# A two-part network on one core: the 32 left-over tokens as the first expert tile, in full fp32 in four strips of one bank, with a new written-out order of all engines' work

## The reference, cut to what matters

```python
x = x + conv_block(layernorm_over_channels(x), ...)      # space gate from Gs, channel gate from Gc
t = tokens(x)                                            # 784 tokens of 128 channels per image
def ffn(x, router_w, router_b, expert_w, expert_b):      # x: layernorm of t
    router_probs = softmax(x @ router_w + router_b)
    top_p, top_i = top_k(router_probs, 2)
    top_p = top_p / sum(top_p)
    expert_out = einsum('bnd,edc->bnec', x, expert_w) + expert_b     # 8 experts, 128 -> 128
    return sum over the two chosen of top_p * expert_out
t = t + ffn(...)
```

## Time and profile before

| what | before |
|---|---|
| median of 3 runs | 1960.88 us (1959.79 to 1966.5) |
| the profiled execution | 1958.27 us, its span 1956.5 us |
| granted TensorE clock, mean | 0.986 |
| busy: PE, PEld | 1779.4 us (91%), 1301.2 us (67%) |
| busy: DVE, ACT, POOL | 1502.8 us (77%), 1195.2 us (61%), 1131.6 us (58%) |
| DVE idle before the first gate of a unit, in the step shown below | 3.04 us |

### The profile page before, as it was taken

One profiled execution on the slowest core, in us unless ns is written; L12 is line 12 of the kernel. 1 busy time (PEld: TensorE's weight loads), 2 busy tenths in 40 slices (PEclk: granted clock), 3 DMA queues, 4 the chain that ended last, 5 costly groups with the idle time before them and its releaser, 6 DMA issues.

```text
span 1956.5 us, 38711 instructions
## 1 busy us (share of the span) xinstructions
PE 1779.4 (91%) x13076; PEld 1301.2 (67%) x13076; DVE 1502.8 (77%) x4703; ACT 1195.2 (61%) x3346; POOL 1131.6 (58%) x1268
## 2 busy tenths in 40 slices
PE   4889999999999999999999999999999999998996
PEld 3467667667666666666766766666766676666764
DVE  4458778788777788777778877778877778877666
ACT  3446656566666666665656665666666666666554
POOL 1134557575556666556666555667555666655565
PEclk9799999999999999999999999999999999999998
DMA  4111121212222211222121222121222221121111
GB/s 126 50 67 51 67 84 67 75 57 70 77 74 70 81 59 67 76 67 84 67 70 57 75 67 83 67 84 51 76 73 70 74 77 62 64 75 51 50 51 50
DMA packets 56177, 135.13 MB, mean 69 GB/s; under 512 B 16268, under 2 KB 18333, under 8 KB 55982
## 3 DMA queue, kind: packets, MB, share of 16 engines
q1 hardware_dynamic: 55320, 130.81, 19.6%
q10 hardware_dynamic: 662, 1.84, 0.3%
HBM read 106.50 MB, written 26.13 MB: 68 GB/s over the span
## 4 chain that ended last, share of the span: by engine, by line
PE 47%; POOL 29%; ACT 13%; DVE 6%; issue 4%; DMA 1%; SPq 0%; POOLq 0%; ACTq 0%; DVEq 0%
POOL part L559 8%; ACT part L795 7%; POOL x1l L544 6%; POOL rstd L508 5%; POOL otok L564 5%; DVE part L1663 4%; PE high L1233 3%; PE high L1235 3%; PE high L1234 3%; PE rot L1056 3%; PE rot L1043 3%; PE rot L1186 2%; PE low L1233 2%; PE rot L1057 2%; ACT tok L646 2%
## 5 line engine op out<-in xcount | busy, mean ns | idle before, releaser
L559 POOL TENSOR_TENSOR part<-part 128x256 f32<-128x256 f32 (+1 forms) x416 | 332.0, 798 | 445.8 <-DVE part L1663 445.7
L795 ACT ACTIVATE part<-low,gv 128x128 f32<-128x128 f32 (+1 forms) x1664 | 460.1, 393 | 164.8 <-PE low L1235 81.6
L1663 DVE SCALAR_TENSOR_TENSOR part<-high,gv,part 128x128 f32<-128x128 f32 (+1 forms) x1664 | 452.1, 339 | 122.3 <-ACT part L795 100.0
L1087 PE MATMUL rot<-x1h,wch 128*128 128x256 f32 x960 | 237.3, 287 | 0.0
L564 POOL TENSOR_TENSOR otok<-part 128x128 f32<-128x128 f32 (+1 forms) x416 | 212.8, 512 | 32.6
L1088 PE MATMUL rot<-x1h,wcl 128*128 128x256 f32 x960 | 228.3, 278 | 0.0
L526 POOL TENSOR_TENSOR tp_l<-tp,tp_h 128x448 fp32r<-128x448 f32 x64 | 66.1, 1032 | 247.5 <-ACT tp_h L675 245.0
L1087 PEld LDWEIGHTS rot<-x1h,wch 128*128 128x128 f32 x960 | 180.9, 188 | 10.0 <-issue 9.4
L1233 PE MATMUL high<-weh,xh 128*128 128x512 f32 (+1 forms) x416 | 178.4, 429 | 8.6 <-DVE part L1663 8.5
L1233 PE MATMUL low<-weh,xh 128*128 128x512 f32 (+1 forms) x416 | 179.1, 431 | 3.5 <-ACT part L795 3.2
L1088 PEld LDWEIGHTS rot<-x1h,wcl 128*128 128x128 f32 x960 | 181.1, 189 | 0.1
(11 more groups left out here) (242 smaller groups left out, 4072.2 us busy)
## 6 DMA issues: line engine op xcount, KB each, us to landing
xin<-in_x SPq DMA_DIRECT2D x32, 784.0 KB, 4.3
x<-in_x SPq DMA_DIRECT2D x32, 784.0 KB, 4.4
cen<-shift_rows SPq DMA_DIRECT2D x32, 784.0 KB, 4.3
out<-x SPq DMA_DIRECT2D x64, 392.0 KB, 2.4
y_ch<-rstd_rows SPq DMA_DIRECT2D x32, 768.0 KB, 3.8
otok<-in_ggs_w SPq DMA_DIRECT2D x1, 600.2 KB
tok<-in_ggs_w SPq DMA_DIRECT2D x1, 600.2 KB
rstd_rows<-both_rows SPq DMA_DIRECT2D x32, 7.0 KB
```

The costliest lines, as they stand in the source:

```text
L559: nc.gpsimd.tensor_tensor(part[0:n, slot, 0:2, :], part[0:n, slot, 0:2, :], part[0:n, slot, 2:4, :], ALU.add).then_inc(sem("half_sum"), 1)
L795: last = nc.scalar.activation(part[0:n, turn % RING, e, :], low[turn % 2][0:n, e * C:(e + 1) * C], ACT.Copy, scale=gv[par(p, back)][0:n, i ...
L1087: nc.tensor.matmul(dst, wch[:, j, rows], hi_x, start=(j == 0), stop=False)
L1663: last = nc.vector.scalar_tensor_tensor(out=own, in0=high[turn % 2][0:n, e * C:(e + 1) * C], scalar=gv[par(p, back)][0:n, i, HALF + e:HALF ...
```

## The change

The short tile of 32 tokens becomes the first of a unit, and tiles 0 to 11 follow: place i in the order is tile (i + 12) mod 13 (`tile`). It is no longer made of three rounded products per half: `rest_products` multiplies the unrounded `cen` by `weh` and then by `wel` in full fp32, two experts (256 columns) per product, each pair of experts in its own strip of 32 partitions and columns 0 to 255 of one `low` bank. There is no `high` product for it (`high_filled` counts 12 per unit), both gates read the `low` bank through `rest`, and the next but one low tile waits for `high_gated` too. `x_high` and `x_low` leave these 32 columns out. SP's `shift_in` waits for the unit's product in addition, since `cen` is now read by it. `finish` waits for one tile more.

All the lists are reordered. The table `USES` takes the order of the new PE list, so the rotating banks are dealt in that order (its diff is left out here). In the diff below lines away from a change are left out, and 8 blanks at the start of each line.

```diff
+def tile(i):
+    return (i + TILES - 1) % TILES
+def rest(v, e):
+    return v[32 * (e // 2):32 * (e // 2) + PAIR * S % 128, (e % 2) * C:(e % 2 + 1) * C]
...
+                need(sp, "low_filled", k, p, 1, back + 1)
...
         store(0, 5)
+        rstd_out(1)
         store(1, 5)
+        rstd_in(1)
         load_residual(3)
-        rstd_out(1)
-        rstd_in(1)
         load(0)
...
-                    need(pool, "high_filled", k, p, TILES, back + 2)
+                    need(pool, "high_filled", k, p, TILES - 1, back + 2)
...
-                nc.gpsimd.tensor_tensor(flat(xl[o])[:, span(f)], flat(cen)[:, span(f)],
-                                        flat(xh[o])[:, span(f)].bitcast(F32), ALU.subtract)\
+                own = slice(384 * f, 384 * f + 384)
+                nc.gpsimd.tensor_tensor(flat(xl[o])[:, own], flat(cen)[:, own],
+                                        flat(xh[o])[:, own].bitcast(F32), ALU.subtract)\
...
-                slot, n = count_of(k, p, back, i) % RING, rows(i)
+                t = tile(i)
+                slot, n = count_of(k, p, back, i) % RING, rows(t)
...
-                if i == FLAT[piece(i)][0]:
-                    need(pool, "fin_filled", k, p, piece(i) + 1, back + 1)
-                nc.gpsimd.tensor_tensor(otok[0:n, i, :], part[0:n, slot, 0, :], part[0:n, slot, 1, :],
+                if i == 0 or t == FLAT[piece(t)][0]:
+                    need(pool, "fin_filled", k, p, piece(t) + 1, back + 1)
+                nc.gpsimd.tensor_tensor(otok[0:n, t, :], part[0:n, slot, 0, :], part[0:n, slot, 1, :],
...
         inverse_std2(4)
+        tp_low(1, 2)
         x1_low(0, 3)
+        add_token(7, 5)
         x1_low(1, 3)
-        tp_low(1, 2)
-        add_token(7, 5)
         add_token(8, 5)
...
         add_token(10, 5)
+        add_token(11, 5)
         x_low(0, 4)
-        add_token(11, 5)
         add_token(12, 5)
...
-                    need(act, "high_filled", k, p, TILES, back + 2)
+                    need(act, "high_filled", k, p, TILES - 1, back + 2)
...
-                nc.scalar.copy(flat(xh[par(p, back)])[:, span(f)], flat(cen)[:, span(f)]).then_inc(sem("xh_ready"), 1)
+                own = slice(384 * f, 384 * f + 384)
+                nc.scalar.copy(flat(xh[par(p, back)])[:, own], flat(cen)[:, own]).then_inc(sem("xh_ready"), 1)
...
-                turn, n = count_of(k, p, back, i), rows(i)
+                turn, t = count_of(k, p, back, i), tile(i)
+                n = rows(t)
...
-                    last = nc.scalar.activation(part[0:n, turn % RING, e, :], low[turn % 2][0:n, e * C:(e + 1) * C], ACT.Copy,
-                                                scale=gv[par(p, back)][0:n, i, e:e + 1])
+                    src = rest(low[turn % 2], e) if i == 0 else low[turn % 2][:, e * C:(e + 1) * C]
+                    last = nc.scalar.activation(part[0:n, turn % RING, e, :], src, ACT.Copy,
+                                                scale=gv[par(p, back)][0:n, t, e:e + 1])
...
         gate_low(8, 5)
+        theta_phi(1, 2)
         x_tokens(0, 0, 1)
-        x_tokens(0, 1, 1)
-        x_tokens(1, 0, 1)
-        x_tokens(1, 1, 1)
-        gate_low(9, 5)
-        gate_low(10, 5)
-        theta_phi(1, 2)
-        x1_high(0, 3)
         tp_high(1, 2)
...
             wide_weights(2)
+        gate_low(9, 5)
+        x_tokens(0, 1, 1)
+        gate_low(10, 5)
+        x1_high(0, 3)
+        x_tokens(1, 0, 1)
         shift_copy(4)
...
             wide_weights(3)
+        x_tokens(1, 1, 1)
         x1_high(1, 3)
...
             expert_weights()
+        gate_low(11, 5)
         mix_copy(2)
...
             wide_weights(4)
-        gate_low(11, 5)
         gate_low(12, 5)
         channels(0, 3)
+        joint(0, 0, 0, 2)
         x_high(0, 4)
         x_high(1, 4)
+        joint(0, 0, 1, 2)
         x_high(2, 4)
...
         channels(1, 3)
+        rstd_copy(1)
         logit_copy(4)
-        joint(0, 0, 0, 2)
-        joint(0, 0, 1, 2)
         gram_copy(0, 3)
+        gram_copy(1, 3)
+        router_exp(4)
         channels(2, 3)
-        gram_copy(1, 3)
-        rstd_copy(1)
-        router_exp(4)
         joint_c(3)
...
         gate_low(1, 4)
+        hidden(0, 2)
         joint(1, 0, 0, 2)
         joint(1, 0, 1, 2)
+        gate_low(2, 4)
         channel_exp(3)
-        gate_low(2, 4)
         gate_low(3, 4)
+        joint(1, 1, 0, 2)
+        joint(1, 1, 1, 2)
         gate_low(4, 4)
...
         gate_low(6, 4)
-        joint(1, 1, 0, 2)
-        joint(1, 1, 1, 2)
-        hidden(0, 2)
         hidden(1, 2)
...
-                need(pe, "token_ready", k, p, FLAT[f][1], back)
+                need(pe, "token_ready", k, p, min(FLAT[f][1] + 1, TILES), back)
...
-        def products(dst, i, half, back):
-            o, n = par(p, back), rows(i)
-            tile = slice(128 * i, 128 * i + n)
+        def products(dst, t, half, back):
+            o = par(p, back)
+            cols_t = slice(128 * t, 128 * t + 128)
...
-            nc.tensor.matmul(dst[0:n, :], flat(xh[o])[:, tile], hi_w, start=True, stop=False)
-            nc.tensor.matmul(dst[0:n, :], flat(xh[o])[:, tile], lo_w, start=False, stop=False)
-            return nc.tensor.matmul(dst[0:n, :], flat(xl[o])[:, tile], hi_w, start=False, stop=True)
-        def tile_ready(i, back):
-            if i == FLAT[piece(i)][0]:
-                need(pe, "xh_ready", k, p, piece(i) + 1, back)
-                need(pe, "xl_ready", k, p, piece(i) + 1, back)
+            nc.tensor.matmul(dst[:, :], flat(xh[o])[:, cols_t], hi_w, start=True, stop=False)
+            nc.tensor.matmul(dst[:, :], flat(xh[o])[:, cols_t], lo_w, start=False, stop=False)
+            return nc.tensor.matmul(dst[:, :], flat(xl[o])[:, cols_t], hi_w, start=False, stop=True)
+        def rest_products(dst):
+            for n, w in enumerate((weh, wel)):
+                for g in range(4):
+                    last = nc.tensor.matmul(dst[32 * g:32 * g + 32, 0:2 * C], flat(cen)[:, 128 * (TILES - 1):PAIR * S],
+                                            w[:, 2 * g:2 * g + 2, :].rearrange("p e c -> p (e c)").bitcast(F32),
+                                            start=(n == 0), stop=(n == 1))
+            return last
+        def tile_ready(t, back):
+            if t == FLAT[piece(t)][0]:
+                need(pe, "xh_ready", k, p, piece(t) + 1, back)
+                need(pe, "xl_ready", k, p, piece(t) + 1, back)
...
-                tile_ready(i, back)
...
-                products(low[count_of(k, p, back, i) % 2], i, slice(0, HALF), back).then_inc(sem("low_filled"), 1)
+                if m == 0:
+                    need(pe, "high_gated", k, p, 1, mb)
+                dst = low[count_of(k, p, back, i) % 2]
+                if i == 0:
+                    need(pe, "centred_ready", k, p, 4, back)
+                    rest_products(dst).then_inc(sem("low_filled"), 1)
+                else:
+                    tile_ready(tile(i), back)
+                    products(dst, tile(i), slice(0, HALF), back).then_inc(sem("low_filled"), 1)
...
-                m, mb = ago(i, 2, back)
-                tile_ready(i, back)
+                m, mb = (i - 2, back) if i > 2 else (i + TILES - 3, back + 1)
...
-                products(high[count_of(k, p, back, i) % 2], i, slice(HALF, E), back).then_inc(sem("high_filled"), 1)
+                tile_ready(tile(i), back)
+                products(high[i % 2], tile(i), slice(HALF, E), back).then_inc(sem("high_filled"), 1)
...
         low_half(8, 5)
-        x_tokens(0, 0, 1)
-        high_half(8, 5)
-        x_tokens(0, 1, 1)
-        x_tokens(1, 0, 1)
-        x_tokens(1, 1, 1)
-        low_half(9, 5)
-        low_half(10, 5)
-        finish(1, 5)
         theta_phi(1, 2)
...
             wide_weights(2)
-        low_half(11, 5)
-        shift_turn(4)
-        low_half(12, 5)
+        x_tokens(0, 0, 1)
+        x_tokens(0, 1, 1)
+        low_half(9, 5)
+        finish(1, 5)
         tp_tokens(1, 2)
...
             wide_weights(3)
+        low_half(10, 5)
+        x_tokens(1, 0, 1)
+        high_half(8, 5)
+        low_half(11, 5)
+        shift_turn(4)
+        x_tokens(1, 1, 1)
         high_half(9, 5)
+        low_half(12, 5)
         high_half(10, 5)
...
         channels0_low(3)
+        joint(0, 0, 2)
+        channels(1, 3)
         finish(2, 5)
-        channels(1, 3)
+        rstd_turn(1)
         logits(4)
-        joint(0, 0, 2)
         finish(3, 5)
...
         router(4)
+        high_half(1, 4)
+        high_half(2, 4)
+        gram_turn(3)
         channels(2, 3)
-        rstd_turn(1)
-        gram_turn(3)
-        high_half(0, 4)
-        high_half(1, 4)
         joint_c(3)
...
         low_half(1, 4)
+        hidden(0, 2)
         channel_logit(3)
         joint(1, 0, 2)
-        x1_channels(0, 0, 3)
         low_half(2, 4)
         low_half(3, 4)
-        high_half(2, 4)
         high_half(3, 4)
+        x1_channels(0, 0, 3)
+        joint(1, 1, 2)
         low_half(4, 4)
```

(60 more changed lines are left out.)

## The result

The changed kernel took 2001.6 us in the median of 4 runs (1999.08 to 2003.03), against 1961.86 for the kernel before on the same chip: a ratio of 1.0198 [1.0176, 1.0219]. Forecast was 1886, with 1852 to 1930 as the range. The span of the profiled execution is 2000.4 us.

What follows compares the result with a forecast made beforehand. The bound was taken to be a loop from `finish(3)` through TensorE, ACT and POOL, TensorE's work just below. Step 37.29 + 18.02 + 0.14 = 55.45 us, 2.58 less; over 28 steps plus ends 74 less: 1886 us, range 1852 to 1930.

Steps and rivals of the forecast that it cites:

- The loop and the way to POOL's release: Step set by the chain from `finish(3)` through ACT and POOL back; stretch until POOL starts falls from 38.24 to 37.29 us.
- A: Stretch from `finish(3)` until POOL is let go and starts its work: 37.29 us, from 38.24.
- The tile: Short tile on TensorE: two fp32 rounds cost 1.14 us instead of 1.48, gaining 0.34 a step.
- Rival 4: Strips accumulating in one bank don't run side by side: tile 3.0 us over its price, step 58.4, 1970 us; chance 0.06.
- The pow: POOL's pow of `inverse_std1`, begun before VectorE's `centre_tokens(0)`, takes about 2.6 us, not 3.54; 0.95 us less a step.
- Rivals 2 and 3: Pow keeps 3.5 us, step 56.4, 1912 us, chance 0.20; running pow holds VectorE up, step 56.1, 1905 us, chance 0.08.
- Third, the adds ... +0.3: POOL's last adds: contention with VectorE, counted as 1.6 us before, grows by 0.3 us a step.
- B: POOL's stretch from its release to its last add before `finish(3)`: 18.02 us, from 19.60.
- That hole closes because `joint(0,0)` and `rstd_turn` fill it: TensorE's wait before the logits, 1.68 us before, vanishes; TensorE then idles 1.1 us before `finish(3)`.
- rival 5: A wait placed wrong costs 1 to 2.5 of the 2.6 us gained per step: 1914 to 1957 us; chance 0.12.
- The sum: Whole step: 37.29 + 18.02 + 0.14 = 55.45 us, 2.58 less than before; 1886 us in all.

Runs made afterwards that it cites:

- e1_fill12: Changed kernel plus twelve extra 512-column products with overwritten result, filling TensorE's wait before `finish(3)`; 1950.89 us, ratio 0.9945 to the kernel before.
- e6_scale_early: Changed kernel with one VectorE edit: the second scaling of the tokens, `x1_tokens(1)`, goes ahead of `gate_high(8)`; 1892.58 us, ratio 0.9659 to the kernel before.
- e4_dve: Changed kernel, VectorE reordered: `x1_tokens(1)` ahead of `gate_high(8)`, `centre_tokens(1)` behind the last output addition; 1871.53 us, ratio 0.9535 to the kernel before.
- e3_late: Changed kernel with `finish(3)` moved behind the gram products and router transposes on TensorE; 1931.32 us, ratio 0.9843 to the kernel before.
- e10_pow_back: e4_dve with `centre_tokens(0)` put back in front of the pow, right behind the moments; 1897.63 us, ratio 0.9677 to the kernel before.

## Why the prediction was wrong, step by step

**The loop and the way to POOL's release: right.** In e1_fill12, at full clock, x1l starts at 990.34, 37.14 us after `finish(3)` of the step before, at 953.20; I had 37.29 for A with the start of its work. TensorE idles before the logits no longer, and tp_l stands before x1l, with POOL waiting 0.69 (I said near 0.9).

**The tile: right.** Forecast 1.14 for its two rounds, 1.00 in the chain; gain 0.34 a step forecast, 0.31 measured. Rival 4 (strips one after the other) is out.

**The pow: right.** 2.60, as read from the shortest of the earlier trace rows; 0.95 a step forecast, 0.81 when given back. Rivals 2 and 3 are out: x1l's predecessor on VectorE, `x1_tokens(0)`, takes 1.22 beside a running pow here too (957.14, beside 955.62 + 2.44).

**"Third, the adds ... +0.3": the first step that failed.** This term of B was 2.3 too small. B measures 1010.63 - 990.34 = 20.29 in e1_fill12 against 18.02. I had sized contention by the rows of before, where VectorE and POOL took turns and each add lost some tenths. What the new order brought were two meetings that the trace of before doesn't have, in which one engine stood still for the whole of the other's work: `x1_tokens(1)` behind x1l (1.55 a step by e6_scale_early) and the second half add behind a batch of VectorE operations. I had taken `x1_tokens(1)` for hidden, looking at when its result was wanted and not at which POOL operation it would meet. The Trainium skill, "SBUF — State Buffer", section "Who interferes with whom", has the rule for it: of a VectorE operation with two SBUF inputs and a GpSimd operation that reads SBUF, the one that starts second waits until the first is done. The 2.84 us agree. The 3.24 us agree only in that one engine stood: the add was issued 0.06 us ahead of the batch, not behind it, and it stood for five operations and not for one. In the prediction I weighed that rule against the pow alone, where the trace went against it, and let it go for the rest; it bears on every pair.

**"That hole closes because `joint(0,0)` and `rstd_turn` fill it": the second.** Closing it was right, and I gave TensorE 1.1 us of idle time before `finish(3)` as harmless. With B late by 2.3 this became one wait of 3.1, which I had taken at its face value: as time that costs what it lasts. It also took the clock: 3.0 or 1.6 us more for the next stretch, 2.2 in the mean of the steps. Without the clock the time would have been about 1940 by the steps, or 1951 as e1_fill12 took it, which rival 5 (a misplaced wait, 1914 to 1957) still holds. None of my rivals had the clock fall, though the earlier trace rows together showed that TensorE could idle 3.25 in two pieces and keep full speed, and only that. The Trainium skill, "TensorE: Matmul & The Clock Gate", section "What's actually happening", says that TensorE, once left idle, goes back from 2.4 to 1.2 GHz; the trace agrees (0.50 from 982 to 986 us, behind the wait of 3.14).

**The sum:** 55.45 + 2.0 (lock, net) + 2.2 (clock) = 59.65, against 59.64. In time: 1886 + 28 x 2.0 + 28 x 2.2 = 2004, against 2001.6. With the clock held and most of the lock gone, as in e4_dve (its half add still takes 2.37), the step is 55.01 and the time 1871.53, at the lower end of the forecast's own range (1868 to 1901).

**What stays open:** why POOL's half add waits for a whole batch in one case and takes turns with it in the other. What goes with the one or the other here is when the batch starts. In the changed kernel and the nine experiments in which the batch meets that add, from 300 to 1750 us, it starts 0.05 to 0.07 us behind the add in 247 steps, and the add is held in all of them; it starts 0.08 to 0.11 us behind it in 9 steps, at most one a kernel, and they take turns in all of them. In the kernel before, the batch started 0.9 us behind the start of POOL's L559 and they took turns at 3.33 us. Being held isn't dear in every order: in e4_dve the one step with a free add takes 54.56 against 55.01. Open is also what decides whether a piece of 1.6 us brings the fall: before, two of that length a step brought one in 28 steps, in e3_late one a step brought 15.

## What to carry to other kernels

When an order is found with fixed durations, check two things that such a search can't see: for every pair of VectorE and GpSimd operations that come to overlap, who is held and for how long; and how TensorE's idle time is cut up, since one piece of 3 us cost 1.6 or 3.0 us more and two of 1.6 nothing in all but one step. A meeting of VectorE and GpSimd can turn on some hundredths of a us (0.07 and 0.08 here), so an order should keep them apart and not rest on who comes first. Removing a wait of TensorE isn't a gain if it joins the next one; work that can be put between two waits (e3_late: one line, 70 us) is worth more there than in front of both. And where a time moves the wrong way with TensorE busier than before, read the granted clock before the chain.

## What the runs showed that I had not expected

- Idle pieces of TensorE ahead of `finish(3)` and falls between 187 and 1737 us (26 to 28 steps): 0.48 us, none; 1.28 (e10_pow_back), none; 1.32, one; 1.63, 15; 1.95, 23; 2.64, 22; 3.14, 25. The half clock lasted 3.4 or 6.8 us, over work that kept TensorE busy.
- Whether a half add took 0.46 us or was held for 2.4 to 3.2 went with some 0.02 us in where VectorE's batch started: at most 0.07 us behind the add, or from 0.08 on.
- Twelve products for nothing made the kernel 51 us faster; four did nothing.
- A half add of 0.46 us took 3.24, and a scaling of 0.94 took 2.84, each standing until the other engine's work was done.
- A pow begun 0.05 us behind a VectorE operation took 3.64; begun 1.3 us ahead of it (969.31 against 970.58), 2.60, and VectorE's 1.22 stayed.
